# A two-layer kernel with a mixture of experts: routing of the first three samples dispatched early, the last sample's between expert blocks

## The chip, the cores and the metric

The kernel runs on one core of one Trainium2 chip. The metric is device time in microseconds (us) of one execution. Three runs of the kernel before gave 983.07, 977.55 and 981.09 us, median 981.09.

## What is computed

The input is x, 4 samples of 32 by 32 positions with 256 channels, so 4 x 1024 = 4096 tokens. All of it is float32.

```python
# layer 0: non-local block on each sample, 32 features
theta, phi, g = xf @ W_theta + b_theta, xf @ W_phi + b_phi, xf @ W_g + b_g
x = x + softmax(theta @ phi.T) @ g @ W_out + b_out
# layer 1a: Nystrom attention, 8 heads of 32, 128 landmarks, on t = layernorm(x)
q_l, k_l = means of q and k over runs of 8 tokens
attn = softmax(q k_l.T) @ (pinv(softmax(q_l k_l.T)) @ (softmax(q_l k.T) @ v))   # pinv: 6 iterations
t = t + attn @ w_out.T + b_out
# layer 1b: mixture of 16 experts on layernorm(t), the best 2 for each token
probs = softmax(xf @ W_gate);  top_g, top_i = top_k(probs, 2)
y = sum over the two picks of  top_g * (gelu(xf @ W1[e]) @ W2[e])     # 256 -> 512 -> 256
t = t + y
```

The number of tokens that each expert gets follows from the inputs. Over all four samples it is 269, 371, 331, 470, 957, 915, 584, 865, 786, 425, 263, 770, 232, 441, 313, 200 for experts 0 to 15; over the first three samples alone 221, 285, 242, 373, 703, 665, 451, 696, 577, 333, 203, 515, 171, 332, 230, 147.

## The kernel before, in words

**Passes.** The four samples go one after the other through four passes (i = 0 to 3). A pass has three stages of eight tiles of 128 tokens, one tile in a slot. Stage 1 is layer 0's attention, stage 2 is the landmark side of layer 1 (with the inverse, cut in pieces that run between its slots), stage 3 is the token side. In each slot TensorE (PE) makes scores, turns probabilities and multiplies values; VectorE (DVE) takes the row maxima (`maxima`, L1249) and the norms; ScalarE (ACT) takes exponentials (L1107, L1112) and copies turned probabilities (L1120). In stage 3 `turn_inverses` (L707) spreads the eight reciprocals of a tile's head sums over partitions by eight small matmuls with a broadcast column of `head_inv` as weights, against the identity. `rows1` adds a tile's result to `t` (L1420), takes its moments, GpSimd (POOL) turns the variance into a factor (L404, L405), `norm1` writes the normed row (L1391).

**Routing.** The gate of sample i - 1 is multiplied early in stage 1 of pass i (`turn_high`, `gate` L612, `gate_turned` L621). The two largest logits of each token, their expert numbers, one-hot masks and running counts (`top_two` L1314, `index` L1320, `picks`, `one_hots` L1337, `either` L1347, `counted` L1354) are made by DVE in slots 0 to 7 of stage 2.

**Between the passes and the blocks.** The last sample has no next pass. After its stage 3 come, with nothing beside them, its gate, its routing, counts over all samples, the rank of each pick within its expert's list (bf16 matmuls L979 to L985), and `select`/`place`: eight rounds in which DVE and ACT make one-hot masks (L1665, L1667, L1184, L1175) and PE multiplies them (L995) into a table that says for each of 79 blocks and 128 rows which token stands there. Then the tables are read out, four gathers are issued, and the blocks begin.

**Blocks.** 79 blocks of 128 rows (`BLOCKS` = 2 x 4096/128 + 15), sorted by expert, the rest empty under expert 15. For block n: POOL gathers 128 normed rows with their gates from DRAM by an indirect DMA (`gather`, L441) into one of 4 buffers; PE turns them (`turn_rows`), DVE copies them (L1714); ACT copies the expert's first weights (`stage_w1`, L1198); PE multiplies (`hidden`, L1026), ACT takes the gelu (L1207), PE multiplies again (`rows_out`, L1035), DVE weighs by the gate (L1731) and POOL adds the rows to the output in DRAM by an indirect DMA (L455). PE's order in an iteration is `hidden(n+1)`, `turn_rows(n+2)`, `rows_out(n)`.

**What orders the additions.** Two experts may add to one token's row, so the additions of different experts must not overlap. The first eight blocks wait each for the one before to land (L454). Later, block n waits for all blocks before the first block of its own expert; the SP queue waits for these landings by a table `release` and counts up `scatter_ok`, on which POOL waits. Blocks of one expert do not wait for each other. POOL's order is gather(n+4), the waits, addition n.

**Experts' weights.** SP loads 32 pieces of 512 KB: 20 in stages 1 to 3 of the last pass (buffers of the passes lie where the rest go), 12 after the last sample is done. ACT waits for all 32 before its first copy.

## Time and profile before

| | |
|---|---|
| profiled execution, its own time | 984.38 us |
| its span, first to last instruction | 982.5 us |
| median of three runs | 981.09 us |
| mean granted TensorE clock | 0.962 of full speed |
| busy share of the span | PE 92%, PE weight loads 71%, DVE 57%, ACT 46%, POOL 30% |
| chain that ended last | PE 77%, DVE 12%, issue 4%, ACT 3%, DMA 2%, POOL 1% |
| DMA | 50.80 MB in 47865 packets, mean 52 GB/s |

The page of the profile gives busy times of each engine and cuts the span in 40 slices of 24.6 us, each digit the busy share in tenths. PEld are the weight loads of PE, which run beside its matmuls. A line number such as L1026 is that of the kernel's source. "Idle before" is the time in which the engine did nothing ahead of an instruction, with what ended it.

### The profile page before, as it was taken

How to read it: one execution, taken by the hardware profiler on the slowest of the kernel's cores; microseconds unless marked ns; L12 is line 12 of the kernel's file. 1: busy time of each engine (PE TensorE's matmuls, PEld its weight loads, DVE VectorE, ACT ScalarE, POOL GpSimd, SP SyncE). 2: the span in 40 equal slices, each digit the busy share in tenths (PEclk: the TensorE clock that was granted, in tenths of full speed). 3: DMA queues.
4: the chain of work that ended last, by engine and by line, in shares of the span. 5: the costliest groups of instructions: out<-in, count | busy, mean ns of one | idle time of the engine just before them, and what ended most of it. 6: DMA issues, size and time to landing. Idle time of an engine off the chain costs nothing.

```text
span 982.5 us, 21960 instructions
## 1 busy us (share of the span) xinstructions
PE 902.8 (92%) x7133; PEld 700.9 (71%) x7135; DVE 558.1 (57%) x1577; ACT 449.2 (46%) x1009; POOL 298.0 (30%) x343
## 2 busy tenths in 40 slices
PE   6999989899989899999899999539999999999997
PEld 4666767566767565767556667428889999999996
DVE  3677847677857587857678775693222222222221
ACT  3524376524367443349443348244434444444441
POOL 2240002050001060001130000103567667666764
PEclk8899999999999899999899999858999999999999
DMA  3100000300000300000206004671344444434431
GB/s 107 45 1 2 1 2 33 98 1 1 1 1 24 108 1 1 1 2 2 87 1 214 1 1 152 180 228 40 53 67 69 67 69 65 72 57 69 64 61 18
DMA packets 47865, 50.80 MB, mean 52 GB/s; under 512 B 11088, under 2 KB 41168, under 8 KB 47792
## 3 DMA queue, kind: packets, MB, share of 16 engines
q0 software_dynamic: 15168, 18.85, 12.0%
q1 hardware_dynamic: 31344, 30.86, 9.9%
q8 instruction: 44, 0.72, 0.3%
q10 hardware_dynamic: 1280, 0.13, 0.1%
q14 instruction: 29, 0.24, 0.1%
HBM read 33.00 MB, written 18.78 MB: 53 GB/s over the span
## 4 chain that ended last, share of the span: by engine, by line
PE 77%; DVE 12%; issue 4%; ACT 3%; DMA 2%; POOL 1%; ACTq 0%; POOLq 0%; DVEq 0%
PE PS L1026 14%; PE PS L1035 13%; PE PS L549 12%; PE PS L889 7%; PE PS L578 6%; PE PS L641 3%; PE PS L747 3%; PE PS L652 3%; PE PS L646 3%; DVE neg_max L1249 3%; PE PS L728 3%; PE PS L733 2%; ACT arena L1112 1%; PE PS L742 1%; DVE arena L1237 1%
## 5 line engine op out<-in xcount | busy, mean ns | idle before, releaser
L404 POOL TENSOR_SCALAR aggr<-aggr 128x1 f32<-128x1 f32 x64 | 14.2, 222 | 510.6 <-DVE aggr L1388 510.6
L1249 DVE TENSOR_REDUCE neg_max<-PS 128x1 f32<-128x1024 f32 (+1 forms) x96 | 117.5, 1224 | 75.0 <-PE PS L652 27.3
L1026 PEld LDWEIGHTS PS<-low 128*128 128x128 f32 x1264 | 153.0, 192 | 5.5 <-DVE low L1714 1.7
L1026 PE MATMUL PS<-low 128*128 128x128 f32 x1264 | 154.2, 275 | 0.4 <-DVE low L1714 0.4
L1035 PE MATMUL PS<-arena,low 128*128 x632 | 150.2, 381 | 2.7 <-ACT low L1207 1.8
L549 PE MATMUL PS<-ident,arena 128*128 128x128 f32 x1008 | 139.5, 285 | 12.8 <-ACT arena L1107 5.4
L455 POOL DMA_INDIRECT out_dram<-low,row_of x79 | 125.4, 1587 | 82.5 <-DVE low L1731 27.6
L549 PEld LDWEIGHTS PS<-ident,arena 128*128 128x128 f32 x1008 | 121.4, 149 | 38.7 <-issue 29.8
L1120 ACT COPY arena<-PS 128x1024 f32<-128x1024 f32 x96 | 98.3, 1024 | 87.3 <-PE PS L549 87.3
L1035 PEld LDWEIGHTS PS<-arena,low 128*128 128x128 f32 x632 | 114.0, 190 | 16.9 <-issue 4.6
L1207 ACT ACTIVATE low<-PS 128x512 f32<-128x512 f32 x79 | 47.2, 597 | 158.5 <-PE PS L1026 139.7
L1107 ACT ACTIVATE arena<-PS,neg_max 128x1024 f32<-128x1024 f32 x64 | 71.3, 1114 | 85.6 <-DVE neg_max L1249 85.6
L441 POOL DMA_INDIRECT low<-rows_scratch,token_of x79 | 78.1, 988 | 64.2 <-DVE token_of L1687 38.7
L1112 ACT ACTIVATE arena<-PS,neg_max 128x128 f32<-128x128 f32 x256 | 90.1, 396 | 7.7 <-DVE neg_max L1249 7.7
L1198 ACT COPY low<-arena 128x1024 f32 x79 | 82.5, 1045 | 18.5 <-issue 14.7
L1731 DVE TENSOR_SCALAR low<-PS,slot_gate 128x256 f32<-128x256 f32 x79 | 38.2, 484 | 91.4 <-issue 61.5
L1712 DVE TENSOR_TENSOR gate_parts<-low,pick_of 128x2 f32<-128x2 f32 x79 | 12.8, 161 | 131.8 <-PE PS L549 122.4
L889 PE MATMUL PS<-arena 128*128 128x256 f32 x320 | 74.4, 386 | 0.0
L578 PE MATMUL PS<-arena,low 128*128 128x512 f32 x128 | 64.6, 630 | 6.9 <-DMA bias_col<-in_L_conv_b_phi_dram 3.3
L889 PEld LDWEIGHTS PS<-arena 128*128 128x128 f32 x320 | 59.1, 190 | 11.2 <-issue 4.0
L1073 ACT ACTIVATE arena<-PS 128x512 f32<-128x512 f32 x40 | 23.8, 595 | 84.1 <-PE PS L578 40.2
L1112 ACT ACTIVATION_READ_ACCUMULATOR arena<-PS,neg_max 128x1 f32 x256 | 60.4, 236 | 0.0
(217 smaller groups left out, 1312.8 us busy)
## 6 DMA issues: line engine op xcount, KB each, us to landing
arena<-in_L_ffn_W_dram SPq DMA_DIRECT2D x32, 512.0 KB, 8.0
out_dram<-t SPq DMA_DIRECT2D x4, 1024.0 KB, 7.4
arena<-in_x_dram SPq DMA_DIRECT2D x3, 1024.0 KB, 6.4
rows_scratch<-arena SPq DMA_DIRECT2D x4, 512.0 KB, 3.6
rows_scratch<-arena SPq DMA_DIRECT2D x8, 256.0 KB, 2.8
low<-rows_scratch,token_of POOLq DMA_INDIRECT x79
out_dram<-low,row_of POOLq DMA_INDIRECT x79
arena<-in_x_dram SPq DMA_DIRECT2D x2, 512.0 KB, 4.9
```

The source lines that it names most:

```text
L441: pool.indirect_dma_start(xg[:, n % 4, :], None, rows_dram, bass.IndirectOffsetOnAxis(ap=token_of[:, n:n + 1], axis=0)).then_inc(xg_loaded ...
L455: pool.indirect_dma_start(out_rows, bass.IndirectOffsetOnAxis(ap=row_of[:, n:n + 1], axis=0), y_sb[:, n % 4, :], None, bounds_check=T - 1, ...
L549: mm = pe.transpose(PS[0:s.shape[1], dst_bank, n * P:n * P + s.shape[0]], s, ident[0:s.shape[0], 0:s.shape[0]])
L578: mm = pe.matmul(PS[0:m, bank, :], w[c], src[:, c, half * 512:half * 512 + 512], start=c == 0, stop=c == KC - 1)
L889: mm = pe.matmul(bank[:, o:o + 2 * M], RX[:, g, h, 0, :], RX[:, g, h].rearrange("p r m -> p (r m)"), start=True, stop=True)
L1026: mm = pe.matmul(PS[:, 2 + p, hc * P:(hc + 1) * P], w1_now[:, p, c * H + hc * P:c * H + (hc + 1) * P], xgT[:, p, c, :], start=c == 0, stop ...
L1035: mm = pe.matmul(PS[:, 6 + p, 0:D], hT[:, p, c, :], w2_sb[:, bass.ds(e * (HC * D) + c * D, D)], start=c == 0, stop=c == HC - 1)
L1107: act.activation(Pm[:, u % 2, :], src, ACT.Exp, bias=neg_max[:, u % 2, 0:1], accum_out=row_sum[:, u % NT:u % NT + 1]).then_inc(s_exp, 1)
L1112: ins = act.activation(Pm[:, u % 2, o:o + M], src[:, o:o + M], ACT.Exp, bias=neg_max[:, u % 2, h:h + 1], accum_out=head_sum[:, u % 2, h:h ...
L1120: act.copy(PT[:, u % 2, :], PS[:, 2:4, :].rearrange("p b n -> p (b n)")).then_inc(t_act, 1)
L1198: act.copy(w1_now[:, p, :], w1_sb[:, bass.ds(e * (KC * H), KC * H)]).then_inc(w1_staged, 1)
L1249: dve.tensor_reduce(dst, src, AX.X, ALU.max, negate=True).then_inc(s_max, 1)
```

## The change

It has these parts.

1. **Routing of samples 0 to 2 in stage 1.** `top_two`, `index`, `picks`/`keep`/`one_hots`, `either`/`counted` of sample i - 1 move from slots 0 to 7 of stage 2 to slots 3 to 6 of stage 1 of pass i (`route`), for i = 1 to 3.
2. **Lists in DRAM.** In pass i >= 1 PE makes the ranks of sample i - 1 (`ranks`, 2 to 7 bf16 matmuls) between the value and key projections, DVE turns them into places (`ranks_out`, `places`), and POOL scatters the pick numbers by 16 indirect DMAs of 128 four-byte cells a sample (`scatter_cells`) into `cells_dram`, a list for each expert.
3. **First part of the blocks.** Each expert's full blocks of samples 0 to 2 (40 in all, `SURE` = 32 of them certain whatever the data) come first. In stages 2 and 3 of the last pass their lists are gathered, turned and made into tables (`early_starts`, `early_blocks`, `early_cells`, `early_tables`), their gates stored, and the gathers of blocks 0 to 3 issued in slots 4 to 7 of stage 3.
4. **Blocks begin after the last tile.** Right after the last `finish` PE starts `hidden(0)`. The last sample's gate, routing, ranks, and its one-hot masks for 48 columns run as pieces (`aside`) between blocks 0 and 19, which are unrolled (`OPEN` = 5 rounds of 4). Its remaining blocks (leftover rows of each expert with the last sample's) follow as blocks 40 to 78, again in order of expert. `select` and `place` are gone.
5. **PE's order in a block** is `turn_rows(n+2)`, `hidden(n+1)`, `rows_out(n)`, in all 79.
6. **Stage 3.** POOL spreads the reciprocals by two broadcast copies (`spread_inverses`) and `turn_inverses` is two transposes. `rows1` and `norm1` stand ahead of `out_t`, and the moments are taken in two steps around `maxima`.
7. **Buffers and loads.** Buffers of the passes are laid out anew so that experts 0 to 8 (both weights) load in the last pass, the rest at its end and beside the first blocks. A block waits for its own expert's weights (`experts_loaded` counts experts in order).

```diff
+                def route(s):
+                    if s == 3:
+                        for t in range(NT):
+                            top_two(i, t)
+                    elif s == 4:
+                        for t in range(NT):
+                            index(i, t)
+                    elif s == 5:
+                        picks(i)
+                        keep(i)
+                        one_hots(i)
+                    elif s == 6:
+                        either(i)
+                        counted(i)
...
+            def scatter_cells(j):
+                pool.wait_ge(places_ready, j + 1)
+                if j == 0:
+                    pool.wait_ge(cells_cleared, 16 * 2)
+                for n in range(j * 2 * NT, (j + 1) * 2 * NT):
+                    pool.indirect_dma_start(cells_dram, bass.IndirectOffsetOnAxis(ap=place_i[:, n:n + 1], axis=0),
+                                            pick_no[:, n:n + 1], None).then_inc(cells_written, 16)
...
+                def spread_inverses(t):
+                    pool.wait_ge(inv_ready, i * NT + t + 1)
+                    if t >= 2:
+                        pool.wait_ge(inv_mm, i * NT + t - 1)
+                    by_place = head_inv[:, t % 2, :].rearrange("p (a g b) -> p g a b", g=NG, b=2)
+                    for g in range(NG):
+                        pool.tensor_copy(inv_spread[:, t % 2, g * P:(g + 1) * P].rearrange("p (a b d) -> p a b d", a=2, b=2),
+                                         by_place[:, g].unsqueeze(3).broadcast_to([P, 2, 2, HD])).then_inc(inv_spread_ready, 1)
+                for t in range(NT + 3):
+                    if t < NT:
+                        spread_inverses(t)
+                    if t >= 3:
+                        pool.wait_ge(x2_done, i * NT + t - 3 + 1)
+                        apart(pool, "pool")
+                        deviation(t - 3, i).then_inc(dev2_ready, 1)
+                    if i == B - 1 and t == NT - 4:
+                        pool.wait_ge(tokens_ready, 1)
+                        pool.wait_ge(gates_stored, 16)
+                        pool.wait_ge(xn2_stored, 16 * 3 * (B - 1))
+                        pool.wait_ge(q_mm, B * 4)
+                    if i == B - 1 and NT - 4 <= t < NT:
+                        gather(t - (NT - 4))
...
-                    for g in range(NG):
-                        for j in range(QUADS):
-                            h = g * GH + j
-                            mm = pe.matmul(PS[HD * j:HD * j + HD, 0, g * P:(g + 1) * P], head_inv[:, t % 2, PLACE[h]:PLACE[h] + 1].broadcast_to([P, HD]),
-                                           ident[:], start=True, stop=True, tile_position=(0, HD * j))
-                    mm.then_inc(inv_mm, 1)
+                    transposes(pe, 0, [inv_spread[:, t % 2, g * P:(g + 1) * P] for g in range(NG)]).then_inc(inv_mm, 1)
...
+                def ranks():
+                    pe.wait_ge(routed, i * ROUTE)
+                    pe.wait_ge(pr_used, i * UNITS + NT)
+                    upto, mine = PS[:, 1, 0:E * NT], slice(E * NT * i, E * NT * (i + 1))
+                    pe.matmul(upto, below_h[:], both[:, mine], start=True, stop=False)
+                    for j in range(i - 1):
+                        pe.matmul(upto, ones_h[:], sample_total(j).unsqueeze(2).broadcast_to([P, E, NT]), start=False, stop=False)
+                    mm = pe.matmul(upto, ones_h[:], cum[:, mine], start=False, stop=True)
...
+            aside = {1: lambda: turn_high(B - 1), 3: lambda: gate(B - 1), 4: lambda: gate_turned(B - 1), 8: late_ranks,
+                     15: lambda: late_place(0), 16: late_turns, 17: lambda: late_place(1)}
             def expert_block(i, u, again=True):
                 p = u % 2
                 n = i * 4 + u
+                if ahead(i, u, 2):
+                    turn_rows((u + 2) % 4, i + (u + 2) // 4, p)
                 if ahead(i, u, 1):
                     hidden(n + 1, 1 - p, again or u >= 1)
-                if ahead(i, u, 2):
-                    turn_rows((u + 2) % 4, i + (u + 2) // 4, p)
                 rows_out(n, p, expert(n))
...
+            aside = {2: lambda: bulk(23, xT[:, 1, 512:1024], j=B - 1), 8: late_exps, 13: late_gates_out}
...
+            aside = {0: lambda: releases(0, IN_TURN, release_early[:, IN_TURN:SURE]), 2: lambda: bulk(22, xT[:, 0, 512:1024], j=B - 1),
+                     4: lambda: gate_out(B - 1), 5: late_top, 6: late_index, 7: late_picks, 8: late_counts, 9: late_starts,
+                     10: late_blocks, 11: late_gates, 12: late_run, 14: lambda: late_hots(0), 15: lambda: late_hots(1),
+                     18: late_tables, 19: lambda: releases(1, SURE, release_late[:])}
```

The three `aside` tables are those of PE, ACT and DVE: the key is the block after (PE, ACT) or in (DVE) whose turn the piece stands. On DVE a piece stands after `rows_turned(n+2)` and before block n's weighing (L1731 before).

## Rows read from the trace of the kernel before

**Rows 1.** Page of the profile: PE's busy share in 40 slices of the span.
```profile
PE   6999989899989899999899999539999999999997
```
**Rows 2.** Two stretches: us, then busy us (instructions) of each engine, PEclk, DMA, GB/s.
```profile
629.00:674.00 45.00, 21.38 (x133) 16.32 (x134) 33.48 (x115) 16.57 (x39) 4.12 (x4) 0.54 0.62 186
760.00:972.00 212.00, 211.69 (x1473) 198.76 (x1472) 59.20 (x225) 90.90 (x111) 143.47 (x112) 1.00 0.40 63
```
**Rows 3.** Timeline (start, us, engine, line): PE's last attention product, first and last of the blocks.
```profile
625.38 1.03 PE L747 MATMUL PS<-low 128*128 128x256 f32 x4
...
674.24 1.94 PE L1026 MATMUL PS<-low 128*128 128x128 f32 x15 [0.37 <-DVE low L1714]
...
971.93 3.62 PE L1035 MATMUL PS<-arena,low 128*128 x16
```
**Rows 4.** Timeline, DVE: routing of the last sample, first and last steps and the gates between.
```profile
634.79 0.17 DVE L1314 MAX8 top_now<-logits_now 128x8 f32<-128x16 f32 x1
...
635.87 0.22 DVE L1614 TENSOR_TENSOR gates<-top 128x64 f32<-128x64 f32 x1
...
636.61 0.08 DVE L1320 MATCH_VALUE_LOAD top_i<-top_now,logits_now 128x8 f32 x1
...
639.77 0.42 DVE L1354 TENSOR_TENSOR_SCAN cum<-restart,both 128x128 bf16<-128x128 bf16 x1
```
**Rows 5.** Timeline, DVE in stage 1 of the last pass: maxima of two slots running.
```profile
500.72 1.23 DVE L1249 TENSOR_REDUCE neg_max<-PS 128x1 f32<-128x1024 f32 x1
...
503.85 1.23 DVE L1249 TENSOR_REDUCE neg_max<-PS 128x1 f32<-128x1024 f32 x1
```
**Rows 6.** Timeline of one slot of stage 3.
```profile
609.60 1.05 ACT L1120 COPY arena<-PS 128x1024 f32<-128x1024 f32 x1
609.84 0.46 PEld L707 LDWEIGHTS PS<-ident,head_inv 128*32 128x32 f32 x16
...
610.86 0.37 ACT L1112 ACTIVATE arena<-PS,neg_max 128x128 f32<-128x128 f32 x1 [0.21 <-DVE neg_max L1249]
...
611.25 1.01 PEld L549 LDWEIGHTS PS<-ident,arena 128*128 128x128 f32 x8
611.40 0.19 DVE L1365 RECIPROCAL head_inv<-head_sum 128x8 f32<-128x8 f32 x1
...
613.61 1.05 ACT L1120 COPY arena<-PS 128x1024 f32<-128x1024 f32 x1
```
**Rows 7.** Timeline of one block in the steady stretch.
```profile
853.37 1.95 PE L1026 MATMUL PS<-low 128*128 128x128 f32 x16
...
854.94 1.59 POOL L455 DMA_INDIRECT out_dram<-low,row_of  x1 [0.74 <-issue]
...
856.84 0.99 POOL L441 DMA_INDIRECT low<-rows_scratch,token_of  x1 [0.30 <-issue]
857.11 1.95 PE L1026 MATMUL PS<-low 128*128 128x128 f32 x16
```
**Rows 8.** Timeline, POOL and PE: additions that wait and one that does not.
```profile
709.23 1.59 POOL L455 DMA_INDIRECT out_dram<-low,row_of  x1 [1.81 <-DMA out_dram<-low,row_of]
...
713.92 1.59 POOL L455 DMA_INDIRECT out_dram<-low,row_of  x1 [1.81 <-DVE low L1731]
...
715.81 0.99 POOL L441 DMA_INDIRECT low<-rows_scratch,token_of  x1 [0.30 <-issue]
...
717.11 1.59 POOL L455 DMA_INDIRECT out_dram<-low,row_of  x1 [0.30 <-issue]
...
718.89 0.44 PE L549 MATMUL PS<-ident,low 128*128 128x128 f32 x2 [0.15 <-DMA low<-rows_scratch,token_of]
```
**Rows 9.** The chain of waits (start, us): a gate in a pass; timeline: one masked product.
```profile
490.25 0.86 PE PS L612 x16
...
662.76 0.93 PEld L995 LDWEIGHTS PS<-low 128*128 128x128 bf16 x8 [1.16 <-DVE low L1667]
```
**Rows 10.** Timeline, POOL: the first gather, issued while DVE works on the tables.
```profile
667.54 1.24 POOL L441 DMA_INDIRECT low<-rows_scratch,token_of  x1 [38.70 <-DVE token_of L1687]
```

More of the change, by code:

```diff
@@ L432, in _ @@
                     add_bias(i + 1)
-                for t in range(NT):
-                    pool.wait_ge(x2_done, i * NT + t + 1)
-                    apart(pool, "pool")
-                    deviation(t, i).then_inc(dev2_ready, 1)
+                if i >= 1:
+                    scatter_cells(i - 1)
+                if i == B - 1:
+                    pool.wait_ge(starts_made, 1)
+                    pool.wait_ge(cells_written, 16 * 2 * EARLY)
+                    gather_cells(0, early_cells_in)
@@ new lines, in store_rows @@
+            def store_rows(i, first, last):
+                sp.wait_ge(xn2_ready, i * NT + last)
+                sp.dma_start(of_sample(rows_dram, i)[:, first:last, 0:D], xn[:, first:last]).then_inc(xn2_stored, 16)
+            for i in range(B - 1):
+                sp.wait_ge(s_mm, i * UNITS + 3)
+                sp.wait_ge(x_loaded, (i + 1) * 16)
+                sp.wait_ge(bulk_mm, mm_count(i, UNIT_ORDER[0]) - 1)
+                sp.wait_ge(xb_ready, i + 1)
+                load_x(i + 1)
@@ new lines, in _ @@
+            both_in(4, 5)
+            sp.wait_ge(y_head_mm, B)
+            both_in(6, 7, 8)
+            store_rows(i, 0, 4)
+            loaded(range(9))
+            sp.wait_ge(s_mm, B * UNITS)
+            both_in(9)
+            first_in(10)
+            sp.wait_ge(t_mm, B * UNITS)
+            first_in(11)
+            first_in(12)
+            sp.wait_ge(ot_ready, B * UNITS)
+            second_in(10)
+            second_in(11)
+            second_in(12)
+            store_rows(i, 4, 6)
@@ new lines, in _, with landings @@
+            sp.wait_ge(pr_used, B * UNITS)
+            sp.wait_ge(x2_done, B * NT)
+            first_in(13)
+            first_in(14)
+            store_rows(i, 6, NT)
+            store_out(i)
+            sp.wait_ge(xn2_stored, 16 * 3 * B)
+            sp.wait_ge(bulk_mm, mm_count(i, UNIT_ORDER[-1]))
+            second_in(13)
+            second_in(14)
+            sp.wait_ge(gate_mm, 2 * i + 1)
+            both_in(15)
+            loaded(range(9, E))
+            def landings(release, count):
+                with sp.Fori(0, count) as n:
+                    landed = [sp.value_load(release[0:1, bass.ds(n, 1), u:u + 1].rearrange("p o u -> p (o u)"), min_val=16,
+                                            max_val=16 * (ROUNDS + 1)) for u in range(4)]
+                    for u in range(4):
+                        sp.wait_ge(y_stored[u], landed[u])
+                    sp.sem_inc(scatter_ok, 1)
@@ L830, in _ @@
                 value_rows(13)
+                if i >= 1:
+                    ranks()
                 bulk_done(7)
@@ L1149, in _ @@
                         query_rows(s)
+                    if i == B - 1 and s == 4:
+                        act.wait_ge(probs_in, 1)
+                        act.activation(probs_a, probs_a, ACT.Exp)
+                        act.activation(gates[:, 0:EARLY], gates[:, 0:EARLY], ACT.Exp).then_inc(probs_exp, 1)
                 for s in range(NT):
@@ L1589, in _ @@
                     phi_out(i + 1, 0)
+                else:
+                    dve.wait_ge(tables_ready, 1)
+                    for n in range(2):
+                        rows_turned(n, n, n, 6 + n)
                 rows1(NT - 1)
@@ new lines, in late_top, with late_index, late_picks @@
+            def late_top():
+                logits_out(B - 1)
+                for t in range(NT):
+                    top_two(B, t)
+            def late_index():
+                for t in range(NT):
+                    index(B, t)
+                dve.wait_ge(routed, (B - 1) * ROUTE + NT)
+                keep(B)
+            def late_picks():
+                picks(B)
+                one_hots(B)
+                dve.wait_ge(kept, B)
+                gates_in(probs_b, late, slice(EARLY, TT))
```

736 lines of the change are left out of this document (432 added, 304 removed).

## The prediction, made before the changed kernel was built or run

> **What bounds the kernel now.** I read the page first: PE's slices are 8 and 9 tenths throughout, save a dip to 5 and 3 in the slices at about 614 to 663 us [rows 1]. So there is a long stretch in which PE is the pace, and one hole. The stretches table prices the hole: from 629 to 674 us PE is busy 21.4 of 45 us, its granted clock is 0.54 (mostly the 1.2 GHz level), and DVE, with 33.5 us, is the engine that works; from 760 to 972 us PE is busy 211.7 of 212 us at the full clock (2.4 GHz) and DVE only 59 us [rows 2]. The timeline gives its edges: the last attention product ends at 626.4, the first expert product starts at 674.24 [rows 3]. Nothing else is worth tens of microseconds, so the question is what of these 47.8 us the change gives back elsewhere. For that I read a slot of stage 1, a slot of stage 3, a block, and POOL's queue beside it.
>
> **1. The hole goes.** The new PE order after the last product is two row turns and `hidden(0)`. Two turns are four transposes; eight take 1.01 us of weight loading [rows 6], so 0.5 us. Tables, gathers 0 to 3 and experts 0 to 8 are due before that, on engines that have room in stages 2 and 3. Start of the blocks: 626.4 + 0.5 = 626.9 instead of 674.24, **-47.3 us**. What could be late is ACT (one copy of weights, 1.05 us, right after its last copy of the pass) and DVE's `rows_turned(0)` and `(1)`; both fit before or within 1 us. If experts 0 to 8 are late, this is the term that shrinks (a rival below).
>
> **2. Routing moves into stage 1.** The same instructions for one sample stand in the hole: from the first maximum at 634.79 to the end of the scan at 640.19 are 5.40 us, less 0.74 us for the gates' steps between (635.87 to 636.61) = 4.66 us of DVE time [rows 4]. In stage 2, where they stood, DVE waited for PE in each slot and they cost nothing, so taking them out returns nothing. In stage 1 a slot is 3.13 us and DVE goes from one slot's last step to the next maximum with no idle time before it [rows 5]: there DVE is a bound. PE is about as full there, but it can't run ahead, since its scores wait for exponentials that wait for maxima. So 4.66 us of DVE work a pass come out nearly whole; about 0.4 us may lie in a first slot that still waits for PE. I take 4.3 x 3 passes (i = 1 to 3) = **+12.9 us**. Bounds: 0 if PE is the true bound and DVE has hidden slack, 3 x 4.66 = 14.0.
>
> **3. Ranks in the passes.** PE gets 2, 3 and 7 bf16 products. A bf16 weight load of 128x128 takes 0.93/8 = 0.12 us [rows 9]; with the moving side 0.13 to 0.15 each, 12 of them = **+1.6 us** (0 to 3). DVE's `ranks_out` stands before a wait of DVE for PE, `places` in stage 2 takes the room that the routing left. POOL's 16 scatters a sample take 16 x (0.99 + 0.30) = 21 us by the gather's row or 16 x (1.59 + 0.30) = 30 us by the addition's [rows 7]; they begin early in stage 2 and the next thing that POOL owes is in stage 3, over 40 us later. Cost 0; were they 4 us each, stage 3 would wait some 20 us in three passes, but nothing in the rows is near that.
>
> **4. Stage 3.** A slot is 4.01 us (609.60 to 613.61) and PE loads weights without a gap that is not its own; the spread of reciprocals is 0.46 us of it, two transposes are 1.01/4 = 0.25 us, so PE's slot becomes 3.80 us [rows 6]. ACT then binds: 4.01 less its 0.21 us wait is also 3.80, plus what maxima still arrive late. I take 0.16 us in each of 32 slots = **-5.1 us** (bounds: 32 x 0.21 = -6.7, and +3 if the hop over POOL is late). The hop has room: the reciprocal starts at 611.40 and its product comes in the next slot's place of 609.84, at 613.85, some 2.3 us after the reciprocal ends; two POOL copies are under 1 us. In the last pass gathers of 0.99 + 0.30 us also stand in that queue and use the room up.
>
> **5. Pieces between the blocks.** On PE: eight transposes 1.0, gate 0.86, two transposes 0.3, late ranks 0.4, two masked products of eight loads 2 x 0.93 [rows 9], two turns 0.35 (with 0.4 for their starts) = **+5.2 us** (4.5 to 7). On DVE a block leaves about 2.4 us between the turned rows and its weighing; the longest pieces (masks, tables) are near 3 us, so a few additions are issued up to 1 us late. Hidden from PE by themselves, they enter the next term.
>
> **6. POOL's queue, the price of two passes over the experts.** Steady state: PE's iteration is 857.11 - 853.37 = 3.73 us (3.733 over the stretch). The addition for the iteration that ended at 853.37 starts at 854.94, 5.3 us after that iteration began (849.64), and the next gather at 856.84 [rows 7]. If an addition must wait for the one before it to land, starts are 713.92 - 709.23 = 4.69 us apart; without a wait POOL can follow at 717.11 - 713.92 = 3.19 to 3.22 us. A gather feeds PE about 3.1 us after its start (715.81 to 718.89) [rows 8]. So each change of expert puts the queue 4.69 - 3.73 = 0.96 us further behind and each other block takes back 3.73 - 3.22 = 0.51 us. How far behind may it be? The gather after addition n is for block n+5. It is in at addition + 1.9 + 3.1 = 5.0 us; the addition normally starts 5.3 us after iteration n begins. The old order needs the rows 1.8 us into iteration n+3, at 13.0: slack 2.7 us. The new order turns rows first, at 11.2: slack 0.9 us. Now the runs, from the token counts. Before: 3, 3, 3, 4, 8, 8, 5, 7, 7, 4, 3, 7, 2, 4, 3, 8 blocks, 16 changes; after the first eight (all serial) the debt never passes 2.7, and working it block by block gives 4.5 us of stalls, all before block 13. The trace has 301.3 us from 674.24 to 975.55 [rows 3]; 1.9 for `hidden(0)` + 79 x 3.733 + 4.5 = 301.3, so the recurrence holds. After: 1, 2, 1, 2, 5, 5, 3, 5, 4, 2, 1, 4, 1, 2, 1, 1 and then 2, 1, 2, 2, 3, 3, 2, 2, 3, 2, 2, 3, 1, 2, 2, 7: 32 runs. The same recurrence with slack 0.9 gives stalls of 2.9 us in blocks 0 to 19 (the pieces of part 5 absorb 3), 2.6 in 20 to 39 and 8.2 in 40 to 78, 13.8 in all: **+9.3 us** over before. Bounds: 0 if additions land 0.6 us sooner than that row, +16 if gathers take 3.9.
>
> **7. Loads beside the first blocks.** Seven experts (7 MB) now load at the end of the last pass and beside blocks 0 to 5, while the first eight additions go one by one. No row shows an addition beside such a load; between 0 and 2 us each over five. I take **+1.5 us** (0 to 8).
>
> One rule of the Trainium skill speaks against parts 5 and 6. The first gather, issued while DVE turned the tables in SBUF, held POOL for 1.24 us [rows 10]; a gather in the steady stretch holds it 0.99 [rows 7]. The skill's page "SBUF — State Buffer" (section "SBUF: two separate sides") says that GpSimd can't write the descriptors of its DMAs while DVE holds the port pair that they share, as fast copies within SBUF do. By that rule, and the trace agrees in sign, each of some 20 gathers and additions beside the pieces would be 0.25 us longer, up to 5 us more in all. The sum stands without it.
>
> **Sum:** -47.3 + 12.9 + 1.6 - 5.1 + 5.2 + 9.3 + 1.5 = -21.9 us against the profiled execution's own 984.4 (span 982.5), so 962.5. That execution lies 3.3 us above the median of the runs; carried to the median: **959 us**.
>
> **Rivals.**
> - *Little is given back.* PE is the true bound of stage 1 and additions land in time (parts 2 and 6 near their lower ends). For it: PE is also full in stage 1. Against it: no idle time before DVE's maxima [rows 5]. All of both gone: 959 - 12.9 - 9.3 = 937; half: 948.
> - *The queue is worse.* Gathers at 3.9 us, DVE pieces and loads delay it: part 6 at +16, part 7 at +8: 972.
> - *The blocks don't start early* (the change doesn't do what it says). The waits in front of `hidden(0)`, above all experts 0 to 8, counted only in order and after a store, hold it until late loads are through. Against: these 9 MB have the whole last pass. Held for the 22 us that the sum gains, the time is that of before: 981.
> - *Slower.* POOL's loop (addition, its landing, the next gather, rows turned first) sets the pace of all 79 blocks, changes or not, because rows are needed 1.8 us sooner. The steady loop has only 0.9 us to spare [rows 7, 8]. If every block took the serial 4.69 us, the blocks would take 79 x 0.96 - 4.5 = 71 us more instead of 9.3 more: 959 + 62 = 1021. It decides from 0.3 us of stall in every block beyond part 6 (22/79).
>
> **How the numbers follow.** Forecast 0.50, little given back 0.23, worse queue 0.15, late start 0.05, slower 0.05, other 0.02. The range runs from half of the first rival to just past the second: 943 to 975; the forecast's own is 952 to 967. A difference under 0.5% (4.9 us) can't be told from none. The first three cases are all faster: with most of the rest, faster 0.92; same 0.03 and slower 0.05 from the last two.
>
> **What would show it.** The blocks' first L1026-like product should start near 636 us (626.9 + 12.9 + 1.6 - 5.1 = 636.3) and within 1 us of the last attention product, with PEclk at 1.00 there. Stage 1 slots 3 to 6 of passes 1 to 3 should be about 1 us longer each, with PE idle; pass 0 not. Stage 3 slots should be 3.85 us (before 4.01). From blocks 40 on PE should show waits for the gather of 0.3 to 0.9 us at every second run. It would be wrong if stage 1 slots stay 3.13 us, if PE never waits for a gather, or if it waits in runs of one expert.

## The result, and the profile after

The changed kernel takes 992.77 us (median of 4 runs, 988.55 to 1001.57) against 982.08 for the kernel before (4 runs beside it): ratio 1.0103, 95% interval 1.0057 to 1.0149. It is 1% slower; forecast was 959 us, 2.3% faster. The profiled execution of after took 988.55 us (span 986.8), that of before 984.38 (982.5). In set 3 below one run of the kernel before took 1075.67 us at a mean granted clock of 0.82; the ratios leave it out.

The first view to read is PE's busy share, as in [rows 1]. The kernel after:

```profile
PE   6999999988879989888988997997899999999997
```

The hole of [rows 1] (a 5 and a 3) is gone, but PE's slices of 8 and 7 have spread over the passes and the blocks. The edges of the blocks, kernel after, as in [rows 3]: timeline of PE.

```profile
654.80 1.03 PE L898 MATMUL PS<-low 128*128 128x256 f32 x4
656.20 1.02 PE L1164 MATMUL PS<-low 128*128 128x128 f32 x7 [0.37 <-issue]
```

The last attention product ends at 655.83 and the blocks begin 0.37 us later, as forecast. But that end stood at 626.4 in [rows 3]: the passes became 29 us longer. Where they did comes from the starts of DVE's maxima, 24 a pass. Each stage runs from its first maximum to the next stage's; differences are worked out from these starts:

| us | stage 1, passes 1, 2, 3 | stage 2, passes 0 to 3 | stage 3, passes 0, 1, 2 |
|---|---|---|---|
| before | 48.7, 50.0, 50.1 | 51.6 in each | 51.9 in each |
| after | 55.0, 53.1, 50.2 | 53.2, 64.9, 58.7, 61.8 | 49.2 in each |

Stage 1 also varies by what clock it is granted at its start: it is 50.0 us in pass 0 of the kernel before and 53.2 in that of b_route below, with the same instructions. So single slots are compared. Stage 3 is shorter, as forecast. The surprise is stage 2 of passes 1 to 3: 13.4, 7.1 and 10.3 us longer, where pass 0, which has no scatters, is 1.6 longer, all of it in one slot with a granted clock of 0.82 (9.46 us for 7.80). This is such a place in pass 1 of the kernel after (timeline: start, us, engine, line, what it waited for):

```profile
262.47 1.07 PE L697 MATMUL PS<-ident,arena 128*128 128x128 f32 x8
...
263.48 0.95 POOL L464 DMA_INDIRECT cells_scratch<-pick_no,place_i  x1 [0.30 <-issue]
...
266.22 0.42 DVE L1823 COPY arena<-PS 128x256 f32<-128x256 f32 x1 [3.59 <-remote]
...
267.56 1.01 ACT L1287 COPY arena<-PS 128x1024 f32<-128x1024 f32 x1 [7.89 <-remote]
...
267.94 0.72 PE L879 MATMUL PS<-arena 128*32 128x128 f32 x16 [3.35 <-DVE low L1864]
```

The transposes that ACT copies (L697) ended at 263.54; ACT starts at 267.56. The products that DVE copies ended at 262.49; DVE starts at 266.22. Both waits are put down to a remote event: no local instruction ended just before them. L464 is the scatter of cells: 16 of them ran from 244.2 to 264.4, each 0.96 us with 0.30 between (0.99 and 0.30 in the prediction). A second stall, 276 to 281, comes after the last scatter has been issued. The stretches table, kernel after, over both stalls and over the scatters (us, busy time of the engines, PEclk, DMA share, GB/s):

```profile
262.50:268.00 5.50, 2.15 (x18) 1.19 (x21) 1.41 (x6) 0.44 (x1) 1.63 (x2) 1.00 0.01 0
276.00:283.00 7.00, 3.17 (x21) 2.46 (x22) 3.02 (x8) 1.03 (x2) 0.00 (x0) 0.69 0.01 2
```

The DMA engines are idle (0.01), so this is no shortage of bandwidth, and the granted clock fell only in the second, after PE had waited.

What came late is to be seen in the trace's records of semaphore updates, which no view prints. PE raises a semaphore when a group of products is done; the engine that waits starts when that update is recorded, and here the update comes 3 to 5 us after the product's end:

| PE's work, kernel after | ends | update recorded | engine that waits starts |
|---|---|---|---|
| products for DVE (L1064) | 262.49 | 266.19 | DVE 266.22 |
| transposes for ACT (L697) | 263.54 | 267.54 | ACT 267.56 |
| scores for the maxima (L802) | 264.60 | 267.60 | DVE 267.71 |

From 244 to 282 us 18 of 33 such updates of PE are recorded within 0.15 us of the end of their instruction; the others are late or have no record. In a_skew, a kernel below that does not stall, all 45 from 245 to 282 us are. So the work was done and its signal was late. The write packets of the scatters were not late: in pass 1 the last of the 256 (32 bytes each) begins 1.7 us after the last issue in both kernels.

The signals of the scatters themselves come late too. In pass 3 the gather of the lists waits for them:

```profile
588.63 0.95 POOL L464 DMA_INDIRECT cells_scratch<-pick_no,place_i  x1 [0.30 <-issue]
603.74 0.99 POOL L469 DMA_INDIRECT cell_rows<-cells_scratch,block_at_i  x1 [14.15 <-DMA cells_scratch<-pick_no,place_i]
```

The last of these 4-byte scatters, 512 bytes in all, was reported landed 14.15 us after its issue ended, where additions of 128 KB land in about 3.8 from their issue. A late landing alone is not the stall, though. In a_skew, without a stall, the same gather waits 8.20 us:

```profile
573.79 0.96 POOL L464 DMA_INDIRECT cells_scratch<-pick_no,place_i  x1 [0.30 <-issue]
582.95 1.00 POOL L469 DMA_INDIRECT cell_rows<-cells_scratch,block_at_i  x1 [8.20 <-DMA cells_scratch<-pick_no,place_i]
```

In the blocks, the steady stretch of the kernel after (PE, PEld, DVE, ACT, POOL) answers to the second row of [rows 2], where PE was busy 211.7 of 212 us; and PE's waits in the blocks follow:

```profile
780.00:970.00 190.00, 181.80 (x1247) 165.46 (x1246) 47.83 (x192) 78.66 (x96) 123.05 (x96) 1.00 0.38 60
```

```profile
PEld PS L697 <- DMA low<-rows_scratch,token_of: 30.1, 26, 2.6
```

PE now waits for gathers (26 weight loads, 30.1 us, at most 2.6). From the first to the last addition there are 318.1 us, before 295.9: +22.2, where parts 5 to 7 give 16.0.

### The profile page after: what moved, and what is told of

Read it like the earlier page. It is cut to its first block, busy times and chain, and to the rows that moved or that the text cites. A ratio compares the mean times of both kernels' runs of the same rounds, so it can differ in the third digit from the quotient of the medians.

```text
span 986.8 us, 20869 instructions
## 1 busy us (share of the span) xinstructions
PE 889.3 (90%) x6617; PEld 679.6 (69%) x6618; DVE 541.7 (55%) x1585; ACT 439.2 (45%) x981; POOL 366.3 (37%) x457
## 4 chain that ended last, share of the span: by engine, by line
PE 54%; DVE 14%; DMA 13%; issue 11%; POOL 3%; ACT 2%; another core or an unknown queue 1%; POOLq 0%; ACTq 0%; DVEq 0%; SPq 0%
DMA out_dram<-low,row_of 10%; PE PS L697 10%; PE PS L1064 8%; PE PS L729 7%; PE PS L1164 5%; PE PS L1173 5%; DMA low<-rows_scratch,token_of 3%; PE PS L808 3%; DVE neg_max L1417 3%; PE PS L898 2%; PE PS L802 2%; PE PS L879 2%; PE PS L797 2%; POOL out_dram L548 2%; PE PS L884 2%
## 5 line engine op out<-in xcount | busy, mean ns | idle before, releaser
L697 PE MATMUL PS<-ident,arena 128*128 128x128 f32 x1008 | 137.2, 282 | 14.6 <-ACT arena L1287 8.2
L1164 PEld LDWEIGHTS PS<-low 128*128 128x128 f32 x1264 | 147.4, 192 | 0.8 <-issue 0.7
L697 PEld LDWEIGHTS PS<-ident,arena 128*128 128x128 f32 x1008 | 118.7, 147 | 39.7 <-issue 31.3
L511 POOL COPY inv_spread<-head_inv 128x128 f32<-128x128 f32 x64 | 18.0, 310 | 195.4 <-DVE head_inv L1551 195.4
L1064 PE MATMUL PS<-arena 128*128 128x256 f32 x320 | 83.0, 414 | 6.0 <-DVE arena L1824 5.4
L464 POOL DMA_INDIRECT cells_scratch<-pick_no,place_i x48 | 46.6, 970 | 97.0 <-DVE place_i L1635 83.3
L1064 PEld LDWEIGHTS PS<-arena 128*128 128x128 f32 x320 | 64.0, 206 | 21.0 <-DVE arena L1824 6.6
```

The source lines that it names most:

```text
L697: mm = pe.transpose(PS[0:s.shape[1], dst_bank, n * P:n * P + s.shape[0]], s, ident[0:s.shape[0], 0:s.shape[0]])
L1064: mm = pe.matmul(bank[:, o:o + 2 * M], RX[:, g, h, 0, :], RX[:, g, h].rearrange("p r m -> p (r m)"), start=True, stop=True)
L1164: mm = pe.matmul(PS[:, 2 + p, hc * P:(hc + 1) * P], w1_now[:, p, c * H + hc * P:c * H + (hc + 1) * P], xgT[:, p, c, :], start=c == 0, stop ...
```

## The experiments

Eighteen kernels ran in five sets; those of one set ran on one chip, and the sets on chips 11, 11, 7, 0 and 4. That turned out to matter. "Stage 2" is that of passes 1, 2, 3; the base is 51.6 us, or 53.2 where one slot gets the lower clock (7.8 us become 9.5), which happens in single passes of many kernels (a_skew, b_s4 and b_route among them).

**Set 1 (chip 11): are the scatters enough to make the stalls?** Three kernels add 16 indirect DMAs to stage 2 of passes 1 to 3 of the kernel before; `cell_at[p, n]` is 16p + n.

```
+ for n in range(16):   # b_s4
+     indirect_dma_start(cells_dram at cell_at[:, n], ones[:, 0:1])
  # b_s512: rows of 128 floats;  b_g4: a gather of single floats of x
```

> The kernel before, with one thing added: in passes 1 to 3, after the landmark means, GpSimd issues 16 indirect scatters of 128 cells of 4 bytes each into an unused table in DRAM (64 bytes apart), 48 in all. Nothing reads the table; the output is untouched. Theory A (the scatters stall the other engines in stage 2, whatever else the change did): stage 2 of passes 1 to 3 grows from 51.6 us by some 7 to 13 us each as in the changed kernel, the time by 20 to 35 us, to about 1010; DVE and ACT show idle times of 3 to 11 us ended by a remote event in that stage. Theory B (the stalls come of the new order of work or of the longer program, and the scatters are harmless): stage 2 stays within 1 us of 51.6, the time within 3 us of 982.

> As the kernel with 48 added scatters of 4-byte cells, but each row is 512 bytes. If what stalls the engines is the small write (a 4-byte element in DRAM), stage 2 stays near 51.6 us and the time near 982; if it is each indirect DMA with its 128 descriptors, whatever their size, the time is the same as with 4-byte cells (some 1010). Theory B expects 982 here too.

> As the kernel with 48 added scatters of 4-byte cells, but in the other direction: 48 indirect gathers of 128 elements of 4 bytes from the input x into an unused column of SBUF. If the direction matters (writes to DRAM), the time stays near 982; if small elements or the number of indirect DMAs matter, it is that of the scatters (some 1010). Theory B expects 982.

Measured against 982.31: 985.92 (ratio 1.0026, 0.9991 to 1.0061), 985.31 (1.0036, 1.0000 to 1.0072) and 987.07 (1.0042, 1.0005 to 1.0079). Stage 2 is 53.2, 51.6, 51.6; 51.6, 53.2, 51.6; and 51.8 three times. No stalls in any, scatters of b_s4 landing in 2.1 us. By these three alone theory B would be right. Since b_s4 does not stall either, b_s512 and b_g4 say nothing on size or direction. The fourth kernel says otherwise:

```
  if i == B - 1:  scatter_cells(i - 1)      # was: i >= 1
+ in stage 3, behind spread_inverses(t), for 1 <= i < B - 1:
+     two scatters of sample i - 1
```

> The changed kernel, with the scatters of samples 0 and 1 moved out of stage 2 and paced: two in each slot of stage 3 of the same pass (passes 1 and 2), behind the copies that spread the inverses. Sample 2's scatters stay in stage 2 of pass 3. Theory A: the stalls leave stage 2 of passes 1 and 2 (64.9 and 58.7 us become 52 to 53) and stay in pass 3 (some 62); two scatters are 2.5 us of GpSimd in a slot of 3.75, so stage 3 may lose 0 to 5 us a pass, or as much as stage 2 gains if the scatters stall wherever they are; time 975 to 985 if pacing helps, 993 if it only moves the stalls. Theory B: stage 2 keeps its stalls in all three passes, 993 or more.

Measured 986.52 us, ratio to before 1.0026 (0.9985 to 1.0068). Stage 2 is 52.2, 52.2, 64.4, and stage 3, 49.2 without scatters, is 58.4 in pass 1 and 51.1 in pass 2. So the stalls go where the scatters go; theory B, that the order of work or the length of the program makes them, falls for the changed kernel. They are neither gone nor the same: 9.1 and 1.9 us where 12.8 and 6.5 were. And since this kernel stalls on the chip and in the set in which b_s4 does not, neither chip nor set decides alone.

**Set 2 (chip 11): the addresses.** The four kernels are b_s4 with other tables `cell_at`: b_row p + 128n; b_16k 4096p + n; b_lists 4096(p mod 16) + p div 16 + 8n; b_apart 4096(p mod 16) + 16(p div 16) + n.

> The kernel before with 48 unused scatters of 4-byte cells (16 in stage 2 of passes 1 to 3), as in the first of them, where the cells lay 64 bytes apart and each scatter landed in 2.1 us and stalled nobody. Here partition p of scatter n writes cell 128n+p, so the 128 cells of a scatter lie side by side. Theory C (cells of one scatter that share a short stretch of DRAM delay one another, and with them everything else that uses it): landing grows to 5 to 15 us and stage 2 of passes 1 to 3 from 51.6 to 58 to 65 us. Theory D (side by side is harmless; something of the changed kernel itself is needed): landing 2 to 3 us, stage 2 at 51.6 to 53.2 us.

> As before, but partition p writes cell 4096p+n: every two cells of a scatter are a multiple of 16 KB apart, as the lists of two experts are. Theory E (addresses a power of two apart fall on one place of the memory): landing 5 to 15 us and stalls in stage 2 here. Theories C and D: landing near 2.1 us, stage 2 at 51.6 to 53.2 us.

> As before, but with the addresses of the changed kernel: 16 lists, 16 KB apart, in each of which 8 partitions write neighbouring cells. Theory C or E: stalls as in the changed kernel, stage 2 of passes 1 to 3 at 58 to 65 us, landing up to 14 us. Theory D: landing 2 to 3 us, stage 2 at 51.6 to 53.2 us; the addresses have nothing to do with it.

> As the kernel with 16 lists 16 KB apart, but within a list the cells of one scatter are 64 bytes apart. Theory C: no stalls here, landing near 2.1 us. Theory E: stalls as with neighbouring cells. Theory D: none in either.

One run each: 1027.08, 1025.80, 1037.02 and 1026.73 us, before 982.88 beside them. Stage 2 is 64.7, 64.9, 65.2; 65.1, 65.1, 65.3; 68.6, 66.5, 72.9; 65.2, 65.1, 65.4. So 48 unused scatters of 4 bytes a partition, added to the kernel before and nothing else, can cost 43 to 54 us (one run each, but far outside the spread of any kernel here). That is the trigger, shown without anything of the change. b_s4 was not run again in this set, so whether it is the addresses that part b_row from it, or the set, isn't shown. The same view of b_s4 (no stall) and b_row (stalled), waits between 225 and 262 us (us in total, times, longest):

```profile
ACT arena L1133 <- PE PS L562: 11.0, 5, 2.8
```

```profile
ACT arena L1133 <- remote: 12.0, 1, 12.0
DVE largest L1519 <- remote: 9.2, 1, 9.2
...
PEld PS L741 <- issue: 5.6, 6, 2.0
```

In b_s4 ACT waits five times, for its transposes; in b_row it waits 12.0 us once, DVE 9.2, and PE's loads come singly with up to 2 us between and nothing to wait for. The records of updates say what ended ACT's wait: its transposes ended at 238.18, their signal is recorded at 245.86, ACT starts at 245.88. Of PE's 16 updates from 223 to 248 us 8 are on time, in b_s4 all 25 (219 to 245 us). Ahead of PE's own slow loads the profile shows no wait; whether its next instructions came late was not looked into by any run. All four patterns stalled, C's own counterexample (b_apart) too; I read this as theory F of the next set. (The expectation of b_skew says that all four stalled by 13.2 to 13.6 us a pass; b_lists stalled by 17.1, 15.0 and 21.4.)

**Set 3 (chip 7): lists moved apart.** b_skew and b_fix are b_lists and b_apart with 4224 in place of 4096. In the changed kernel one constant does it; a_perm also stores each block's cells in another order.

```
- LIST = T // P
+ LIST = T // P + 1           # a_skew; cell_base: e * LIST * P
+ place = place - 7 * (place >> 3 & 15) + 15 * (place & 7)    # a_perm
```

> The kernel before with the 48 unused scatters, with addresses as in the changed kernel (16 lists, 8 neighbouring cells in each), except that the lists lie 16.5 KB apart instead of 16 KB. Four patterns stalled stage 2 by 13.2 to 13.6 us a pass (128 neighbouring cells; 16 KB apart; and both mixtures), and one did not (64 bytes apart, so 8 KB in one scatter). Theory F (writes of a scatter that all fall on one part of an interleaved memory wait for one another; a scatter must be spread over it): stage 2 at 51.6 to 54 us here, landing 2 to 4 us. Theory C (cells that share 64 bytes): stalls stay, 58 to 65 us.

> As the kernel with lists 16.5 KB apart, and within a list the cells of one scatter are 64 bytes apart. Theories F and C both expect no stall: stage 2 at 51.6 to 53.2 us, landing near 2.1 us. If it stalls as the others, spreading the lists doesn't help and only a dense region of 8 KB does.

> The changed kernel with one number changed: a list is 33 blocks long instead of 32, so two lists lie 16.5 KB apart instead of 16 KB. Theory F: the stalls of stage 2 in passes 1 to 3 (13.4, 7.1, 10.3 us) go, stage 2 becomes 51.6 to 53, the blocks start some 25 to 30 us earlier and the time is 963 to 968, faster than both kernels. Theory C: no change, 990 to 995.

> The changed kernel with lists 16.5 KB apart, and the cells within a block of 128 stored in another order, so that eight consecutive ranks lie 64 bytes apart; four small VectorE instructions are added to the places of each sample (some 1 us in stage 2), the late part compares with a table in the same order. Theory C: the stalls go only here, 963 to 970 where the other kernel stays at 993. Theory F: as with the lists apart alone, plus 0 to 3 us for the added instructions.

Measured: b_skew 984.46 and b_fix 986.07 (one run each), a_skew 967.27 (963.67 to 968.34), a_perm 974.42, before 988.58 in this set (7 runs); ratios 0.9804 (0.9746 to 0.9862) and 0.9867 (0.9808 to 0.9926). Stage 2 of a_skew is 52.2, 52.2, 55.2: no stalls, and the changed kernel without them is faster than before. It looked like proof of F. One thing the order of the cells does change, within this one set: the last landing is recorded 7.1, 4.4 and 7.4 us after the last issue's end in a_skew and 1.2, 1.6 and 1.2 in a_perm. But neither stalls, so late landings alone do not make the stalls. a_perm's added instructions stand in a slot where DVE is late already (8.1 us became 10.4) and cost 2.3 us in passes 1 and 2, 7 us in all, against up to 3 expected.

**Set 4 (chip 0): the other terms.** a_order is a_skew with the two `if ahead` parts of `expert_block` swapped back; b_route is before with `route(s)` behind slots 3 to 6 of stage 1 for i >= 1; b_stage3 is before with `spread_inverses` on POOL and two transposes in `turn_inverses`; b_loads is before with this:

```
+ sp.wait_ge(tables_ready, 1)
+ for e in range(7): copy w1[e] and w2[e] to a table in DRAM   # 14 x 512 KB
```

> The changed kernel with lists 16.5 KB apart, and in the blocks the old order of TensorE: the next block's hidden products first, then the turn of the rows after it. Part 6 of the prediction: rows may then arrive 1.8 us later; by its recurrence the stalls in the blocks fall from 13.8 to 9.1 us, so the time falls by 4.7 us (3 to 7), to some 962, and the waits of TensorE for gathers (41.8 us, 40 times) shrink at changes of expert. If rows late by more than the slack are the same in both orders (the rival: the queue is behind by so much that the order doesn't matter), the time stays within 2 us; if the new order was needed for VectorE's pieces, it gets slower by 1 to 4 us.

> The kernel before with one part of the change alone: the routing of sample i-1 (maxima of eight, indices, one-hots, sums) stands in stage 1 of pass i, behind slots 3 to 6, instead of in stage 2. Part 2 of the prediction: 4.3 us a pass, 12.9 in all, time 995. The trace of the changed kernel suggests 3.15 us a pass: 9.5, time 991 to 992. If the slots grow for another reason (ranks, another memory layout), stage 1 stays at 50 us and the time at 982.

> The kernel before with one part alone: in stage 3 GpSimd spreads the reciprocals and TensorE turns them with two transposes instead of eight small products. Part 4 of the prediction: 0.16 us a slot, 5.1 us in all, time 977. By the trace of the changed kernel a slot is 3.75 instead of 4.01 us and stage 3 is 2.6 us shorter a pass: 10.5 in all, time 972. If the moments split in two steps, which this kernel leaves out, made half of that, a slot is 3.85 to 3.9 us here.

> The kernel before, with 14 copies of 512 KB from the expert weights to an unused table in DRAM, issued when the tables are ready, so that they run beside the first 5 to 8 additions. The expert weights that the blocks use are loaded as before; the output is untouched. Part 7 of the prediction: the first additions start 4.7 us apart; beside the loads 0 to 2 us more each over five of them, 1.5 us in all (0 to 8). By the trace of the changed kernel the first eight gaps are 7.1 us longer than serial ones (8.2, 5.7, 7.3 where 4.7 stood): 5 to 9 us, time 987 to 991. If only gathers of rows just written were late there, the gaps stay 4.6 to 4.8 and the time 982.

Before was 982.11 (13 runs). a_order 961.75 (0.9818, 0.9763 to 0.9873): stage 2 as in a_skew, from first to last addition 312.1 us instead of 316.4, so the old order gives back 4.3 us (4.7 by the recurrence). b_route 996.73 (1.0162, 1.0115 to 1.0209): slots 5 and 6 are 3.67 and 4.16 us for 3.13 and 3.14, and the stage's last step 26.40 for 25.16, 2.8 us a pass or 8.4 in all; the slots are the same in every pass, the last step within 0.4 us. What the median has above that isn't settled: it is 14.6 us over before, while its profiled execution took 990.32 us, 5.9 over that of before. b_stage3 976.83 (0.9967, 0.9928 to 1.0006): slots 3.75 as in the full change, but stage 3 is 50.4 us, 1.5 a pass and not 2.6. b_loads 998.68 (1.0186, 1.0135 to 1.0236). Its first addition and the next (timeline of POOL, b_loads):

```profile
687.71 1.65 POOL L457 DMA_INDIRECT out_dram<-low,row_of  x1 [11.61 <-DVE low L1738]
...
698.56 1.59 POOL L457 DMA_INDIRECT out_dram<-low,row_of  x1 [7.91 <-DMA out_dram<-low,row_of]
```

The gap is 10.85 us for the serial 4.69 of [rows 8], and the first addition is 6.2 us later than before (681.51). Of this, PE waits 3.5 us for the second gather, and then its first 32 products take 6.14 us for 3.84 before, since the granted clock is 0.50 from 678.1 to 681.2 us (1.00 at the same place before):

```profile
677.66 0.69 PE L556 MATMUL PS<-ident,low 128*128 128x128 f32 x2 [3.48 <-DMA low<-rows_scratch,token_of]
678.14 6.14 PE L1033 MATMUL PS<-low 128*128 128x128 f32 x32
```

So a part of the price of the loads is the clock that PE lost while it waited. The forecast of 0 to 2 us for each of five additions was made for a case that no row showed, and it was low.

**Set 5 (chip 4): the mended version again, and loads held.** a_final is a_order, unchanged to the letter. a_held holds the loads of experts 13 to 15:

```
- first_in(13), first_in(14) after x2_done; second_in(13), second_in(14) later
+ sp.wait_ge(y_stored[3], 16); both_in(13, 14)
```

> The changed kernel with lists 16.5 KB apart and the old order of TensorE in the blocks, and the loads of experts 13 and 14 (2 MB) held, with that of expert 15 (1 MB), until the fourth addition has landed. If loads cost additions time only by how many bytes stand before them, the first gaps (8.3, 5.7, 7.2 us) shrink by 2 to 4 us in all and the later ones (4.7, 5.7, 4.6, 4.6) grow by 0 to 3: time 0 to 4 us less than with the loads where they were. If each megabyte costs the same wherever it lies beside the serial additions, no change. If the held loads delay the first waited additions (the ninth on), 2 to 8 us more.

> The changed kernel with the two edits that the runs point to, and nothing else: lists 33 blocks long instead of 32 (no stalls in stage 2) and the old order of TensorE in the blocks (hidden products before the turn of the next rows). It ran with 3 rounds at 961.75 us; here against the same runs of the kernel before as the kernel with held loads. Expected 960 to 964 us, 2% below the kernel before.

a_final took 1011.72 us (6 runs, 1002.04 to 1012.76) and a_held 1009.52 (1009.16 to 1013.49), before 987.57: ratios 1.0222 (1.0175 to 1.0269) and 1.0243 (1.0211 to 1.0275). The program that ran at 961.75 (959.30 to 967.69) in one set runs 50 us slower in the next, each time with all runs of its set within 11 us. Here is ACT in the same piece of work, pass 1, a_order and then a_final:

```profile
250.48 1.01 ACT L1287 COPY arena<-PS 128x1024 f32<-128x1024 f32 x1 [3.16 <-PE PS L697]
...
256.81 1.01 ACT L1287 COPY arena<-PS 128x1024 f32<-128x1024 f32 x1 [2.79 <-PE PS L697]
```

```profile
253.76 1.01 ACT L1287 COPY arena<-PS 128x1024 f32<-128x1024 f32 x1 [3.15 <-issue]
...
271.06 1.01 ACT L1287 COPY arena<-PS 128x1024 f32<-128x1024 f32 x1 [13.78 <-remote]
```

The same two copies are 6.33 us apart in a_order and 17.3 in a_final. Stage 2 is 52.2, 52.2, 55.2 against 67.7, 72.3, 68.0. With that theory F is refuted as I had it: lists 16.5 KB apart don't prevent the stalls. Sets 2 and 3 can't be set against each other, since set and pattern changed together. What decides in a run is open. It isn't the program alone (a_order and a_final are one), nor the chip or set alone (b_s4 and a_paced). Where the tables come to lie in memory and what else uses that memory are left, and a mixture of all these; no run tells them apart.

On the loads the set does answer. Additions 1 to 3 and 5 to 6, a_held and then a_final:

```profile
688.58 1.64 POOL L548 DMA_INDIRECT out_dram<-low,row_of  x1 [3.38 <-DVE low L2039]
696.66 1.58 POOL L548 DMA_INDIRECT out_dram<-low,row_of  x1 [5.15 <-DVE low L2039]
701.47 1.58 POOL L548 DMA_INDIRECT out_dram<-low,row_of  x1 [1.93 <-DMA out_dram<-low,row_of]
...
710.74 1.58 POOL L548 DMA_INDIRECT out_dram<-low,row_of  x1 [1.81 <-DMA out_dram<-low,row_of]
720.50 1.57 POOL L548 DMA_INDIRECT out_dram<-low,row_of  x1 [6.88 <-DMA out_dram<-low,row_of]
```

```profile
692.41 1.64 POOL L548 DMA_INDIRECT out_dram<-low,row_of  x1 [3.38 <-DVE low L2041]
700.54 1.58 POOL L548 DMA_INDIRECT out_dram<-low,row_of  x1 [5.20 <-DMA out_dram<-low,row_of]
708.87 1.58 POOL L548 DMA_INDIRECT out_dram<-low,row_of  x1 [5.45 <-DMA out_dram<-low,row_of]
...
718.08 1.58 POOL L548 DMA_INDIRECT out_dram<-low,row_of  x1 [1.77 <-DMA out_dram<-low,row_of]
724.03 1.57 POOL L548 DMA_INDIRECT out_dram<-low,row_of  x1 [3.08 <-DMA out_dram<-low,row_of]
```

The second gap shrinks from 8.33 to 4.81 us and the fifth grows from 5.95 to 9.76: five gaps are 31.9 and 31.6 us. Held loads cost as much where they land later; whether they cost nothing where no addition is waited for was not tried.

## Why the prediction was wrong

The step that failed is in part 3: the 16 scatters a sample were costed at 0 because POOL had 40 us of room. Their time on POOL was right (16 x 1.26 us) and POOL did have the room. What was missed is that these scatters have a price on engines that don't wait for them: while they are out, and for some us after, PE's signals to DVE and ACT can come 3 to 8 us late. In the set of the first result it is 12.8, 6.5 and 6.6 to 8.3 us in the three passes, over the same stages without stalls in a_skew (52.2, 52.2, and 53.5 or 55.2 by the clock): 26 to 28 us. In set 5 it is some 48, in sets 3 and 4 nothing. This one term turns the sign. With it gone a_skew's profiled execution takes 963.67 us, where the sum against a profiled execution was 962.5. The sentence that "nothing in the rows is near that" was true and no argument: before the change the kernel has no scatter of 4-byte cells to DRAM at all, so the bound should have been taken from both sides, as part 7 did. Why the signals come late stays open.

- **Part 1, the hole: right.** Blocks start 0.37 us after the last product (0.5 forecast). They start at 633.0 in a_skew for 636.3; 656.2 after.
- **Part 2, routing: right in kind, too dear.** Its mark was stage 1 slots near 1 us longer. In the last pass of the kernel after two maxima stand 4.51 us apart for the 3.13 of [rows 5]:

```profile
518.44 1.20 DVE L1417 TENSOR_REDUCE neg_max<-PS 128x1 f32<-128x1024 f32 x1
522.95 1.21 DVE L1417 TENSOR_REDUCE neg_max<-PS 128x1 f32<-128x1024 f32 x1
```

  The whole is 2.8 us a pass (b_route), 8.4 for 12.9 forecast: DVE hid 1.9 of its 4.66 us behind PE and not 0.4. Taking routing out of stage 2 also returned 0.3 us a pass (stage 3's second gap is 10.54 for 10.86 in b_route), which I had at nothing.
- **Part 3, ranks: too cheap.** Slot 6 is 4.51 us for 4.16 in b_route, 0.35 a pass; but `ranks_out` and `places` lengthen two slots of stage 2 by 0.3 each, and the early tables three slots of pass 3 by 1.3 together. Some 4 us (0.35 + 0.6, three times, + 1.3) for 1.6. The forecast looked at PE alone; the larger share is DVE's.
- **Part 4, stage 3: right in sign, too small.** 2.6 us a pass for 1.3. The slot is 3.75 us, not 3.85. b_stage3 alone gives 1.5, the routing 0.3; the last 0.8 is put down to the other edits in that stage, which were not tried singly.
- **Parts 5 and 6, pieces and queue: in the right size.** A masked product of part 5 was priced from [rows 9] at a granted clock of 0.50 (660 to 664 us of before); in the blocks, at full clock, its eight loads take 0.57 us for 0.93, so part 5 was 0.7 too dear. PE waits for gathers, as it should, though by up to 2.6 us where the mark was 0.3 to 0.9; the order's share was 4.7 by the recurrence and 4.3 measured. From first to last addition a_skew has 20.5 us more than before; with the two parts at 14.5, 6 are left for part 7.
- **Part 7, loads: too small.** Some 6 us for 1.5, inside its bounds of 0 to 8; this is what is left when the other two parts are taken off, not a measurement. The first eight gaps of the kernel after are 45.1 us together, before 35.6; that later blocks take a part of these 9.5 us back is inferred.

Of the errors beside the scatters, parts 2 and 4 were too pessimistic by 4.5 and about 5 us, parts 3 and 7 too optimistic by 2.4 and 4.5. Single slots at the lower granted clock add nearly 4 us to a_skew's passes that no part had. All these nearly cancel, so that a_skew comes within 1.2 us of the sum is in part luck. None of the rivals named the scatters. The rule that I cited from the Trainium skill ("SBUF — State Buffer", section "SBUF: two separate sides") would have made issues on POOL longer beside DVE's pieces. Additions of the kernel after took 1544 to 1634 ns over all blocks, those of [rows 7] and [rows 8] 1590, so additions show nothing of it. Five gathers took 1.18 to 1.23 us for 0.99, two of them beside DVE's two pieces of masks. This is the first of the two:

```profile
729.20 0.95 DVE L1985 TENSOR_TENSOR t<-t,vals 128x768 bf16<-128x768 bf16 x1
729.78 1.23 POOL L475 DMA_INDIRECT low<-rows_scratch,token_of  x1 [0.30 <-issue]
```

That agrees with the rule in sign, but it is 1.1 us together and not up to 5.

No version is shown that beats the kernel before in every set. a_order does by 1.8% where no stalls occur and loses 2.2% where they do. b_stage3 has no scatters; it can't be told from before at 0.9967 (0.9928 to 1.0006).

## What to carry to other kernels

A DMA that nobody waits for isn't free until a trace shows one of its kind: a change that adds an access no row resembles (here 4-byte scatters to DRAM) gets a bound on both sides and a run by itself before it is built into a schedule. Run the deciding kernel in another set, and beside its rival in one set, before believing a cause: sets 3 and 4 agreed with the address theory, and a second run of a_order's program refuted it. Loads beside additions that are waited for one by one cost the same in the two places tried. And where a wait is put down to nothing local, the records of semaphore updates tell whether the work or its signal was late.

## What the runs showed of the hardware that was not expected

- 48 indirect scatters of 128 x 4 bytes, 0.96 us each on POOL, made stage 2 of three passes 7 to 21 us longer in some runs (the kernel after, a_final, b_row, b_lists) and not at all in others (b_s4, a_skew, a_order); a_final and a_order are one program. In the stalls DVE and ACT sat idle for up to 14 us at a time, and PE's semaphore updates were recorded up to 8 us after the work had ended (within 0.15 us in a_skew), while the DMA engines were 1% busy.
- Few landings of the scatters are on record where there are stalls: of the 256 of pass 1 there are 94 in the kernel after and 88 in b_row, all 256 in a_skew and b_s4. Whether they or only their records are lost is not shown.
- The last 16 of these scatters had all landed only 14.15 us after the last issue's end in the kernel after and 8.20 in a_skew, which doesn't stall; b_s4's each landed 2.1 us after their issue.
- 7 MB copied beside the first additions moved an addition's start by 6.2 us and lengthened the next gap from 4.69 to 10.85 us.
